# A graph attention layer on one core: the order of small index products among large products

## Chip, cores and metric

The kernel runs on one core of one Trainium2 chip. The metric is the device time of one execution in microseconds (us); lower is better. TensorE multiplies matrices, VectorE and ScalarE work on tiles, GpSimd and SyncE here mostly issue transfers (DMA) between DRAM and the core's memory.

## The reference, cut to what matters

1250 nodes with 512 features, 20000 edges sorted by destination. The part that the change touches prepares three things: per-node products that later steps gather by edge, empty tables in which the edge stage merges its sums, and index rows that say where in a tile of 128 edges the run of one destination ends.

```python
xn = _layernorm(x, axis=-1)
# inside the graph layer, node_feat = xn
x_cat = jnp.concatenate([node_feat[src], node_feat[dst], edge_feat], axis=-1)
r = x_cat @ Wr.T + br
q = (node_feat @ Wq.T + bq).reshape(n, H, D)
k = (r @ Wk.T + bk).reshape(e, H, D)
v = (r @ Wv.T + bv).reshape(e, H, D)
a = jnp.einsum('ehd,ehd->eh', q[dst], k) * scaler
amax = jax.ops.segment_max(a, dst, num_segments=n)
ae = jnp.exp(a - amax[dst])
asum = jax.ops.segment_sum(ae, dst, num_segments=n)
...
out = jax.ops.segment_sum(m, dst, num_segments=n).reshape(n, H * D)
```

After that come linear attention on the same normalised nodes and a ternary feed-forward layer.

## The kernel before, in words

The kernel is a chain of stages, each with its own instruction list for every engine: `prologue`, `edges`, `mix_and_sums`, `gnn_end`, `ffn`. Engines wait for each other only by semaphores. The change is in `prologue` alone.

Wr is used in three parts (for source, destination and edge features). Each part is multiplied with Wk and Wv into one matrix M (`fold(0)`, `fold(1)`, `fold(2)`, 96 matmuls each). All matrices are split into a high and a low half, so each product of a node tile (128 nodes) with 512 columns is 12 matmuls (`product`, L316). After `fold(0)` the loop `source(t)` makes two products for each of the 10 node tiles, with four transposes for a later tile between them (`turn`). In this stretch GpSimd loads 14 blocks of destination numbers (`load_block`, 12 edge tiles each, two buffers), and VectorE and ScalarE count in each edge tile where an edge stands in its run (`rank_group` L528, `sign_group` L430). On the same queue GpSimd clears the four merge tables (`clear_table`, L269) behind blocks 3, 5, 7 and 9.

After `fold(1)` and its eviction to M comes the destination stage, t = 0 to 9. TensorE runs `destination(t)`: a product on Wq for q, one on M for k, one on M for v, in banks 0 to 2 or 3 to 5 by turns. Behind them stand the index products of four groups of four edge tiles, `cuts(k)` for k = 4t to 4t+3: a column that marks run ends times a one-hot row matrix, 128 columns, four to a bank (6 or 7).

```python
            for t in range(NT):
                destination(t)
                for k in range(4 * t, 4 * t + 4):
                    cuts(k)
```

VectorE builds the one-hot matrices in 8 buffers (`onehot[:, i % 8, :]`, L604), so the groups k and k+2 share buffers, and group k waits for `cuts(k - 2)`. Between the groups it adds the biases to q (L610), to k (L616), forms the node's own score (L620, L623), and adds the bias to v (L626). ScalarE copies each group's bank to `cut_out` (L480), for which the store of group k-2 must have landed; GpSimd stores it to `cut_rows` (L282). SyncE stores v and q of the tile (L209, L211); they have two buffers each. At the end come two transposes, their copies, and `fold(2)`. The edge stage starts when all engines are through, GpSimd having waited for the cleared tables.

Of the kernel before, what the change touches and what calls it, by code (L numbers as in the profile page):

```python
# [106 lines left out]
def prologue(nc, x, WqT, bq, Wr, br, WkT, bk, WvT, bv, src_col, dst_col, dst_row, q_table, kv_table, v2_table, merge,  # L107
# [3 lines left out]
    with ExitStack() as ctx:  # L111
        def sb(name, shape, dt=F32):
            return ctx.enter_context(nc.sbuf_tensor(name, shape, dt))

        def sem(name):
            return ctx.enter_context(nc.semaphore(name))
# [31 lines left out]
        seg_end = sb("seg_end", [P, ET])  # L148
        is_end = sb("is_end", [P, ET])
        is_end16 = sb("is_end16", [P, ET], BF16)  # L150
        onehot = sb("onehot", [P, 8, P], BF16)
        cut_out = sb("cut_out", [1, 2, 4 * P])
        ends_out = sb("ends_out", [P, 2, P])
        banks = [ctx.enter_context(nc.psum_tensor(f"bank{i}", [P, D], F32)) for i in range(8)]
# [9 lines left out]
        q_added, kd_added, own_mul, own_sum, v2_added = (  # L164
            sem("q_added"), sem("kd_added"), sem("own_mul"), sem("own_sum"), sem("v2_added"))
        stored = [sem(f"nodes_stored{i}") for i in range(2)]
        tables_out = sem("tables_out")
# [16 lines left out]
        def wr_load(j):  # L184

            return 3 * j + 2 if j < C else (D0 + j - C if j < 2 * C else E0 + j - 2 * C)

        @block.sync
        def _(sp):
# [17 lines left out]
            def store_nodes(t):  # L207
                sp.wait_ge(v2_added, t + 1)
                sp.dma_start(v2_table[t * P:(t + 1) * P, :], v2_out[:, t % 2, :]).then_inc(stored[t % 2], 16)  # L209
                sp.wait_ge(own_sum, t + 1)  # L210
# [33 lines left out]
        def _(pool):  # L244
# [24 lines left out]
            def clear_table(i):  # L269
                pool.dma_start(merge[i].rearrange("(t p) w -> p t w", p=P),  # L270
                               empty[:, :].unsqueeze(1).to_broadcast([P, NT, TROW])).then_inc(tables_out, 16)

            pool.wait_ge(raw_in[(D0 - 3) % SLOTS], raw_landed(D0 - 3))
            pool.wait_ge(consts, 8)
            pool.dma_start(cut_rows[0:1].unsqueeze(0), empty[0:1, 0:1]).then_inc(tables_out, 16)
            for g in range(len(groups)):
                load_block(g)
                if g in (3, 5, 7, 9):
                    clear_table(g // 2 - 1)
            for k, (lo, n) in enumerate(quads):  # L280
                pool.wait_ge(cut_copied, k + 1)
                pool.dma_start(cut_rows[1 + lo * P:1 + (lo + n) * P].unsqueeze(0),  # L282
# [2 lines left out]
            pool.dma_start(end_rows[0:P * P].rearrange("(t e) -> t e", e=P), ends_out[:, 0, :]).then_inc(tables_out, 16)  # L285
            pool.dma_start(end_rows[P * P:EP].rearrange("(t e) -> t e", e=P),
                           ends_out[0:ET - P, 1, :]).then_inc(tables_out, 16)
            pool.wait_ge(tables_out, 16 * (TABLES + 3))
            pool.wait_ge(cut_stored[0], 16 * (-(-len(quads) // 2)))
            pool.wait_ge(cut_stored[1], 16 * (len(quads) // 2))  # L290

# [1 line left out]
        def _(pe):  # L293
# [22 lines left out]
            def product(out, left_hi, left_lo, t, right_hi, right_lo, cols):  # L316
                tile = slice(t * P, (t + 1) * P)
                for c in range(C):
                    pe.matmul(out, left_hi[:, c, tile], right_hi[:, c, cols], start=c == 0, stop=False)
                    pe.matmul(out, left_hi[:, c, tile], right_lo[:, c, cols], start=False, stop=False)  # L320
                for c in range(C):
                    last = pe.matmul(out, left_lo[:, c, tile], right_hi[:, c, cols], start=False, stop=c == C - 1)
                return last
# [20 lines left out]
            def destination(t):  # L344
                b = 3 * (t % 2)
                if t >= 2:
                    pe.wait_ge(q_added, t - 1)
                product(banks[b][:, :], xT_hi, xT_lo, t, Wq_hi, Wq_lo, slice(0, D)).then_inc(nodes_done, 1)
                pe.wait_ge(m_lo, 16)
                if t >= 2:  # L350
                    pe.wait_ge(kd_added, t - 1)
                product(banks[b + 1][:, :], xT_hi, xT_lo, t, M_hi, M_lo, slice(0, D)).then_inc(nodes_done, 1)
                if t >= 2:
                    pe.wait_ge(v2_added, t - 1)
                product(banks[b + 2][:, :], xT_hi, xT_lo, t, M_hi, M_lo, slice(D, 2 * D)).then_inc(nodes_done, 1)

            def cuts(k):
                lo, n = quads[k]
                pe.wait_ge(hot, lo + n)
                if k >= 2:  # L360
                    pe.wait_ge(cut_copied, k - 1)
                for i in range(n):
                    t = lo + i
                    last = pe.matmul(banks[6 + k % 2][0:1, i * P:(i + 1) * P], is_end16[:, t:t + 1], onehot[:, t % 8, :],
                                     start=True, stop=True)
                last.then_inc(cut_done, 1)

# [20 lines left out]
            fold(1)  # L388
            pe.wait_ge(lo_split, split_at(Q0 + C - 1) + 1)
            pe.wait_ge(m_lo, 9)  # L390
            for t in range(NT):
                destination(t)
                for k in range(4 * t, 4 * t + 4):
                    cuts(k)
            pe.wait_ge(cut_copied, len(quads))
            pe.transpose(banks[6][:, 0:P], seg_end[:, 0:P], ident[:, :])
            pe.transpose(banks[6][0:ET - P, P:2 * P], seg_end[:, P:ET], ident[:, :]).then_inc(cut_done, 1)
# [7 lines left out]
        def _(act):  # L405
# [67 lines left out]
            evict(1)  # L473
            split_wr(2 * C)
            split_wr(2 * C + 1)
            for k, (lo, n) in enumerate(quads):
                act.wait_ge(cut_done, k + 1)
                if k >= 2:
                    act.wait_ge(cut_stored[k % 2], 16 * (k // 2))
                act.activation(cut_out[:, k % 2, 0:n * P], banks[6 + k % 2][0:1, 0:n * P], ACT.Copy,  # L480
                               scale=NEG).then_inc(cut_copied, 1)
# [8 lines left out]
        def _(dve):  # L490
# [4 lines left out]
            def split_wr(j):  # L495
                split(wr_load(j), wr_lo[:, j % 2, :], wr_hi[:, j % 2, :])
# [97 lines left out]
            evict(1)  # L594
            split_wr(2 * C)
            split_wr(2 * C + 1)
            for t in range(NT):
                u, b = t % 2, 3 * (t % 2)
                for k in range(4 * t, 4 * t + 4):
                    lo, n = quads[k]  # L600
                    if k >= 2:
                        dve.wait_ge(cut_done, k - 1)
                    for i in range(lo, lo + n):
                        dve.tensor_scalar(onehot[:, i % 8, :], iota_row[:, :], rank[:, i:i + 1], None,  # L604
                                          ALU.is_equal).then_inc(hot, 1)
                    if k == 4 * t:
                        dve.wait_ge(nodes_done, 2 * NT + 3 * t + 1)
                        if t >= 2:
                            dve.wait_ge(stored[u], 16 * (NT // 2) + 32 * (t // 2))
                        dve.tensor_tensor(q_out[:, u, :, 0:DH], banks[b][:, :].rearrange("p (h d) -> p h d", h=H),  # L610
                                          bq_all[:, :].rearrange("p (h d) -> p h d", h=H), ALU.add).then_inc(q_added, 1)
                    if k == 4 * t + 2:
                        dve.wait_ge(nodes_done, 2 * NT + 3 * t + 2)
                        if t >= 1:
                            dve.wait_ge(own_mul, t)
                        dve.tensor_tensor(kd[:, :], banks[b + 1][:, :], bias[:, 0, :], ALU.add).then_inc(kd_added, 1)  # L616
                        dve.wait_ge(kd_added, t + 1)
                        if t >= 1:
                            dve.wait_ge(own_sum, t)
                        dve.tensor_tensor(own[:, :].rearrange("p (h d) -> p h d", h=H), kd[:, :].rearrange("p (h d) -> p h d", h=H),  # L620
                                          q_out[:, u, :, 0:DH], ALU.mult).then_inc(own_mul, 1)
                        dve.wait_ge(own_mul, t + 1)
                        dve.tensor_reduce(q_out[:, u, :, DH], own[:, :].rearrange("p (h d) -> p h d", h=H),  # L623
                                          AX.X, ALU.add).then_inc(own_sum, 1)
                dve.wait_ge(nodes_done, 2 * NT + 3 * t + 3)
                dve.tensor_tensor(v2_out[:, u, :], banks[b + 2][:, :], bias[:, 1, :], ALU.add).then_inc(v2_added, 1)  # L626
            split_wr(2 * C + 2)
            split_wr(2 * C + 3)
            evict(2)
# [1103 lines left out]
```

## Time and profile before

| | before |
|---|---|
| median of 3 runs | 1941.12 us (1935.93 to 1944.87) |
| the profiled execution | 1957.55 us, span in the trace 1955.8 us |
| TensorE busy | 1662.3 us, 85% |
| VectorE busy | 1273.3 us, 65% |
| ScalarE busy | 1027.3 us, 53% |
| GpSimd busy | 737.3 us, 38% |
| mean granted TensorE clock | 0.932 |

Busy time of an engine says how much of the span it had an instruction under way; the granted clock is the share of TensorE's full clock that the chip let it have. Shares over the whole span are means over stages with different limits, so a change in one stage is read from that stage. PE is TensorE, DVE VectorE, ACT ScalarE, POOL GpSimd, SP SyncE.

### The profile page before, as it was taken

What the parts mean: (1) busy time and instruction counts of PE and PEld (TensorE: products, weight loads), DVE (VectorE), ACT (ScalarE), POOL (GpSimd) and SP (SyncE); (2) the same over time, 40 slices, a digit from 0 to 9 for tenths busy, and PEclk for the clock granted to TensorE, in tenths of its full rate; (3) what the DMA queues carried; (4) which work ended last, traced back from release to release, by engine and by line L of the source; (5) the groups of instructions that cost most, each with busy time, mean ns of one, the idle gap of its engine ahead of it and who ended that gap; (6) DMA issues with size and microseconds to landing.
All of it is one profiled execution on the core that took longest, in us unless ns stands there. A gap on an engine that the chain in (4) does not pass through costs nothing. (4 is left out here: it accounts for less than half of the span.)

```text
span 1955.8 us, 25729 instructions
## 1 busy us (share of the span) xinstructions
PE 1662.3 (85%) x7160; PEld 1212.4 (62%) x7162; DVE 1273.3 (65%) x2943; ACT 1027.3 (53%) x3595; POOL 737.3 (38%) x727
## 2 busy tenths in 40 slices
PE   7978877999999999999999999999999467888723
PEld 6756656777777777777777777777776233443411
DVE  6764443777777777777777777777776354432588
ACT  3871111677667776776677667766776233310011
POOL 0101112455555555555555555555554000000033
PEclk9988888999999999999999999999999688999955
DMA  5860004666656666666666666666663423100001
GB/s 172 308 264 33 34 35 134 191 187 208 198 182 193 199 206 191 193 206 196 193 193 204 205 193 193 208 201 193 193 200 121 169 83 124 61 0 1 22 11 42
DMA packets 127102, 300.20 MB, mean 153 GB/s; under 512 B 29088, under 2 KB 50727, under 8 KB 126962
## 3 DMA queue, kind: packets, MB, share of 16 engines
q0 software_dynamic: 66224, 190.99, 28.3%
q1 hardware_dynamic: 60738, 107.59, 19.0%
q8 instruction: 59, 0.97, 0.2%
q14 instruction: 81, 0.66, 0.1%
HBM read 271.40 MB, written 66.58 MB: 173 GB/s over the span
## 5 line engine op out<-in xcount | busy, mean ns | idle before, releaser
L1115 ACT ACTIVATE wv<-vv,expd 128x64 f32<-128x64 f32 x1256 | 316.8, 334 | 3.2 <-ACT expd L1105 0.7
L1127 ACT ACTIVATE old<-old,expd 128x64 f32<-128x64 f32 x1256 | 307.7, 333 | 0.0
L1065 POOL DMA_INDIRECT merge<-new,put_id x157 | 159.8, 1018 | 381.3 <-DVE new L1249 352.4
L1296 PE MATMUL psV<-M_hi,efT_hi 128*128 128x512 f32 x628 | 266.1, 424 | 0.0
L1296 PE MATMUL psK<-M_hi,efT_hi 128*128 128x512 f32 x628 | 250.1, 398 | 6.5 <-ACT efT_hi L1090 6.5
L1297 PE MATMUL psV<-M_lo,efT_hi 128*128 128x512 f32 x628 | 249.8, 398 | 0.0
L1297 PE MATMUL psK<-M_lo,efT_hi 128*128 128x512 f32 x628 | 249.4, 397 | 0.0
L1036 POOL DMA_INDIRECT old<-merge,dst_id x157 | 195.8, 1247 | 49.1 <-issue 47.5
L1302 PE MATMUL psV<-M_hi,efT_lo 128*128 128x512 f32 x628 | 192.1, 407 | 0.0
L1199 DVE TENSOR_TENSOR vv<-psV,kv 128x512 f32<-128x512 f32 x157 | 108.5, 691 | 121.4 <-remote 115.8
L1036 POOL DMA_INDIRECT kv<-kv_table,src_id x157 | 155.0, 987 | 85.5 <-issue 46.9
L1206 DVE TENSOR_TENSOR wv_lo<-wv,wv_hi 128x512 fp32r<-128x512 f32 x157 | 107.9, 687 | 102.6 <-ACT wv_hi L1120 101.3
L1036 POOL DMA_INDIRECT qc<-q_table,dst_id x157 | 155.5, 991 | 47.9 <-issue 46.6
L1302 PE MATMUL psK<-M_hi,efT_lo 128*128 128x512 f32 x628 | 172.2, 396 | 0.0
L1296 PEld LDWEIGHTS psV<-M_hi,efT_hi 128*128 128x128 f32 x628 | 118.5, 189 | 40.3 <-issue 17.1
L1296 PEld LDWEIGHTS psK<-M_hi,efT_hi 128*128 128x128 f32 x628 | 118.9, 189 | 36.2 <-ACT efT_hi L1090 6.9
L1297 PEld LDWEIGHTS psK<-M_lo,efT_hi 128*128 128x128 f32 x628 | 118.8, 189 | 28.6
L1302 PEld LDWEIGHTS psK<-M_hi,efT_lo 128*128 128x128 f32 x628 | 118.5, 189 | 29.0
L1297 PEld LDWEIGHTS psV<-M_lo,efT_hi 128*128 128x128 f32 x628 | 119.1, 190 | 21.8
L1097 ACT ACTIVATE runsT<-psT 128x16 f32<-128x16 f32 (+1 forms) x79 | 14.5, 183 | 220.0 <-PE psT L1335 220.0
L1302 PEld LDWEIGHTS psV<-M_hi,efT_lo 128*128 128x128 f32 x628 | 112.5, 189 | 21.6
L1523 POOL MEMSET onem<- 128x128 f32 x1 | 0.2, 205 | 321.7 <-POOLq L1374 321.7
(261 smaller groups left out, 3200.9 us busy)
## 6 DMA issues: line engine op xcount, KB each, us to landing
efT<-in_ef_turned_dram SPq DMA_DIRECT2D x78, 512.0 KB
merge<-empty POOLq DMA_DIRECT2D x4, 2640.0 KB, 15.0
rows<-merge SPq DMA_DIRECT2D x40, 264.0 KB, 3.7
row_block<-dst_rows POOLq DMA_DIRECT2D x13, 768.0 KB, 7.1
dst_line<-dst_rows SPq DMA_DIRECT2D x78, 128.0 KB
end_line<-end_rows SPq DMA_DIRECT2D x78, 128.0 KB
kv_table<-kv_out SPq DMA_DIRECT2D x10, 512.0 KB, 5.6
raw<-in_L_gnn_Wr_dram SPq DMA_DIRECT2D x12, 256.0 KB, 5.1
```

Source lines behind the costliest of these rows:

```text
L1036: pool.indirect_dma_start(out=out, out_offset=None, in_=table[:, :], in_offset=bass.IndirectOffsetOnAxis(ap=ids[:, t:t + 1], axis=0)).then ...
L1065: pool.indirect_dma_start(out=merge[2 * (p % 2) + u][:, :], out_offset=bass.IndirectOffsetOnAxis(ap=put_id[:, t:t + 1], axis=0), in_=new[p ...
L1097: act.activation(runsT[:, 0:n, :], turned_s[:, 0:n, :], ACT.Copy).then_inc(runs_copied, 1)
L1115: act.activation(wv[:, u, h * DH:(h + 1) * DH], vv[:, u, h * DH:(h + 1) * DH], ACT.Copy, scale=expd[p % 2][:, u, 0, h:h + 1]).then_inc(wv_ ...
L1127: act.activation(rows, rows, ACT.Copy, scale=expd[p % 2][:, u, 1, h:h + 1]).then_inc(old_scaled, 1)
L1199: dve.tensor_tensor(vv[:, u, :], psV[u][:, :], kv[p % 2][:, u, D:2 * D], ALU.add).then_inc(v_added, 1)
L1206: dve.tensor_tensor(wv_lo[:, u, :], wv[:, u, :], wv_hi[:, u, :].bitcast(F32), ALU.subtract).then_inc(wv_lo_ready, 1)
L1296: pe.matmul(out[:, :], efT_hi[b][:, u, c, :], Me_hi[:, c, col:col + D], start=c == 0, stop=False)
L1297: pe.matmul(out[:, :], efT_hi[b][:, u, c, :], Me_lo[:, c, col:col + D], start=False, stop=False)
L1302: last = pe.matmul(out[:, :], efT_lo[b][:, u, c, :], Me_hi[:, c, col:col + D], start=False, stop=c == C - 1)
L1523: pool.memset(onem[:, :], 1.0).then_inc(cst, 1)
```

## The change

Three edits in `prologue`. (1) TensorE's order in the destination stage: the products are dealt out singly, with one or two groups of index products between them, and the q product of tile t+2 is made after the v product of tile t. (2) The one-hot rows have 16 buffers, four groups, and VectorE's order follows: a group waits for the group four before it. Two semaphores of the own score become one. (3) The four table clears are issued by ScalarE on its own DMA queue, ahead of the copies of groups 0, 6, 12 and 18, with a semaphore of their own.

```diff
-        onehot = sb("onehot", [P, 8, P], BF16)
+        onehot = sb("onehot", [P, 16, P], BF16)
...
+        def destination_at(kind, t):
+            before = 2 * NT + 2 * t + min(t + 2, NT)
+            return {"q": 2 * NT + t + 1 + 2 * max(t - 1, 0), "k": before + 1, "v": before + 2}[kind]
...
             for g in range(len(groups)):
                 load_block(g)
-                if g in (3, 5, 7, 9):
-                    clear_table(g // 2 - 1)
...
-            pool.wait_ge(tables_out, 16 * (TABLES + 3))
+            pool.wait_ge(tables_out, 16 * 3)
+            pool.wait_ge(cleared, 16 * TABLES)
...
-            for t in range(NT):
-                destination(t)
-                for k in range(4 * t, 4 * t + 4):
-                    cuts(k)
+            destination_q(0)
+            pe.wait_ge(m_lo, 12)
+            destination_q(1)
+            pe.wait_ge(m_lo, 16)
+            for t in range(NT):
+                if t >= 1:
+                    cuts(4 * t - 2)
+                    cuts(4 * t - 1)
+                destination_k(t)
+                cuts(4 * t)
+                destination_v(t)
+                cuts(4 * t + 1)
+                if t + 2 < NT:
+                    destination_q(t + 2)
+            cuts(len(quads) - 2)
+            cuts(len(quads) - 1)
...
+            act.wait_ge(consts, 8)
             for k, (lo, n) in enumerate(quads):
+                if k % 6 == 0 and k // 6 < TABLES:
+                    act.dma_start(merge[k // 6].rearrange("(t p) w -> p t w", p=P),
+                                  empty[:, :].unsqueeze(1).to_broadcast([P, NT, TROW])).then_inc(cleared, 16)
                 act.wait_ge(cut_done, k + 1)
...
+            def one_hots(k):
+                lo, n = quads[k]
+                if k >= 4:
+                    dve.wait_ge(cut_done, k - 3)
...
+            one_hots(0)
+            one_hots(1)
+            add_q(0)
+            one_hots(2)
+            one_hots(3)
+            for t in range(NT):
+                if t + 1 < NT:
+                    add_q(t + 1)
+                own_scores(t)
+                if t + 1 < NT:
+                    one_hots(4 * t + 4)
+                    one_hots(4 * t + 5)
+                add_v2(t)
+                if t + 1 < NT:
+                    one_hots(4 * t + 6)
+                    one_hots(4 * t + 7)
```

`add_q`, `own_scores` and `add_v2` hold the same five VectorE operations as before, each with a wait for its product by the count of `destination_at`; `add_q` and now `add_v2` wait for the stores of tile t-2.

## Rows read from the trace of the kernel before

**Rows 1.** Busy time by stretch: us, then each engine, clock, DMA share, GB/s.

```profile
40.00:80.00 40.00, 39.02 (x185) 32.15 (x184) 29.66 (x134) 26.37 (x114) 4.11 (x6) 1.00 0.64 229
143.75:293.81 150.06, 117.64 (x519) 89.43 (x520) 69.50 (x216) 25.20 (x48) 19.34 (x40) 0.84 0.10 34
```

**Rows 2.** Waits, 149 to 293 us: total us, times, longest.

```profile
DVE onehot L604 <- PE bank L364: 42.7, 10, 4.5
...
PE bank L364 <- DVE onehot L604: 31.3, 20, 2.4
```

**Rows 3.** Timeline of TensorE between tiles 0 and 1: start us, us.

```profile
154.49 0.61 PE L364 MATMUL bank<-onehot,is_end 128*1 128x128 bf16 x8
...
158.67 0.39 PE L364 MATMUL bank<-onehot,is_end 128*1 128x128 bf16 x4 [2.44 <-DVE onehot L604]
158.98 0.79 PE L319 MATMUL bank<-Wq_hi,xT_hi 128*128 128x512 f32 x1
```

**Rows 4.** Groups by line, 149 to 293 us.

```profile
L604 DVE TENSOR_SCALAR onehot<-iota_row,rank 128x128 bf16<-128x128 f32 x157 | 34.1, 280 | 42.7 <-PE bank L364 42.7
L319 PE MATMUL bank<-M_hi,xT_hi 128*128 128x512 f32 x80 | 31.6, 395 | 0.0
...
L319 PE MATMUL bank<-Wq_hi,xT_hi 128*128 128x512 f32 x36 | 23.0, 640 | 0.0
L480 ACT ACTIVATE cut_out<-bank 1x512 f32<-1x512 f32 (+1 forms) x40 | 22.0, 574 | 123.8 <-PE bank L364 105.6 <-DMA cut_rows<-cut_out 18.2
...
L282 POOL DMA_DIRECT2D cut_rows<-cut_out x40 | 19.3, 485 | 136.3 <-ACT cut_out L480 136.2
...
L610 DVE TENSOR_TENSOR q_out<-bank,bq_all 128x512 f32<-128x512 f32 x10 | 6.9, 690 | 35.7 <-PE bank L322 35.7
```

**Rows 5.** Waits, 55 to 149 us.

```profile
DVE junk L534 <- DMA row_block<-dst_rows: 12.8, 5, 5.8
...
PE bank L319 <- DVE xT_lo L525: 4.7, 1, 4.7
```

**Rows 6.** Transfers: KB each, us to landing; windows 60:150, 57:62 twice, 98:104 twice.

```profile
merge<-empty POOLq DMA_DIRECT2D x4, 2640.0 KB, 15.0
...
row_block<-dst_rows POOLq DMA_DIRECT2D x1, 768.0 KB, 6.0
kv_table<-kv_out SPq DMA_DIRECT2D x1, 512.0 KB, 3.2
...
row_block<-dst_rows POOLq DMA_DIRECT2D x1, 768.0 KB, 10.8
kv_table<-kv_out SPq DMA_DIRECT2D x1, 512.0 KB, 8.5
```

**Rows 7.** Timeline of TensorE, source stage to the first destination products.

```profile
76.33 0.60 PE L331 MATMUL bank<-ident,raw 128*128 128x128 f32 x4
...
82.23 0.60 PE L331 MATMUL bank<-ident,raw 128*128 128x128 f32 x4
...
94.62 0.60 PE L331 MATMUL bank<-ident,raw 128*128 128x128 f32 x4
...
105.98 0.39 PE L305 MATMUL bank<-W_hi,wr_hi 128*128 128x512 f32 x1
...
143.78 0.76 PE L319 MATMUL bank<-Wq_hi,xT_hi 128*128 128x512 f32 x1 [9.48 <-DVE M_lo L502]
...
148.92 0.40 PE L319 MATMUL bank<-M_hi,xT_hi 128*128 128x512 f32 x1
```

**Rows 8.** Stores of the destination stage and its end on the timeline.

```profile
q_table<-q_out SPq DMA_DIRECT2D x10, 260.0 KB, 2.4
...
cut_rows<-cut_out POOLq DMA_DIRECT2D x39, 2.0 KB, 1.5
...
291.83 0.22 PE L364 MATMUL bank<-onehot,is_end 128*1 128x128 bf16 x1 [1.86 <-DVE onehot L604]
...
293.81 0.76 PE L305 MATMUL bank<-W_hi,wr_hi 128*128 128x512 f32 x1 [0.72 <-ACT ends_out L484]
```

More of the change, by code:

```diff
@@ L163, in prologue @@
         nodes_done, ks_copied, vs_copied = sem("nodes_done"), sem("ks_copied"), sem("vs_copied")
-        q_added, kd_added, own_mul, own_sum, v2_added = (
-            sem("q_added"), sem("kd_added"), sem("own_mul"), sem("own_sum"), sem("v2_added"))
+        q_added, kd_added, own_step, v2_added = sem("q_added"), sem("kd_added"), sem("own_step"), sem("v2_added")
         stored = [sem(f"nodes_stored{i}") for i in range(2)]
-        tables_out = sem("tables_out")
+        tables_out, cleared = sem("tables_out"), sem("cleared")
         block_in = [sem(f"block_in{i}") for i in range(2)]
@@ L209, in store_nodes @@
                 sp.dma_start(v2_table[t * P:(t + 1) * P, :], v2_out[:, t % 2, :]).then_inc(stored[t % 2], 16)
-                sp.wait_ge(own_sum, t + 1)
+                sp.wait_ge(own_step, 2 * t + 2)
                 sp.dma_start(q_table[t * P:(t + 1) * P, :],
@@ L267, in load_block @@
                                dst_rows[lo * P:(lo + n) * P].unsqueeze(0).to_broadcast([P, n * P])).then_inc(block_in[g % 2], 16)
-            def clear_table(i):
-                pool.dma_start(merge[i].rearrange("(t p) w -> p t w", p=P),
-                               empty[:, :].unsqueeze(1).to_broadcast([P, NT, TROW])).then_inc(tables_out, 16)
             pool.wait_ge(raw_in[(D0 - 3) % SLOTS], raw_landed(D0 - 3))
@@ L342, in source, with destination_q, destination_k, destination_v @@
                 product(banks[b + 1][:, :], xT_hi, xT_lo, t, M_hi, M_lo, slice(D, 2 * D)).then_inc(nodes_done, 1)
-            def destination(t):
-                b = 3 * (t % 2)
+            def destination_q(t):
                 if t >= 2:
                     pe.wait_ge(q_added, t - 1)
-                product(banks[b][:, :], xT_hi, xT_lo, t, Wq_hi, Wq_lo, slice(0, D)).then_inc(nodes_done, 1)
-                pe.wait_ge(m_lo, 16)
+                product(banks[3 * (t % 2)][:, :], xT_hi, xT_lo, t, Wq_hi, Wq_lo, slice(0, D)).then_inc(nodes_done, 1)
+            def destination_k(t):
                 if t >= 2:
                     pe.wait_ge(kd_added, t - 1)
-                product(banks[b + 1][:, :], xT_hi, xT_lo, t, M_hi, M_lo, slice(0, D)).then_inc(nodes_done, 1)
+                product(banks[3 * (t % 2) + 1][:, :], xT_hi, xT_lo, t, M_hi, M_lo, slice(0, D)).then_inc(nodes_done, 1)
+            def destination_v(t):
                 if t >= 2:
                     pe.wait_ge(v2_added, t - 1)
-                product(banks[b + 2][:, :], xT_hi, xT_lo, t, M_hi, M_lo, slice(D, 2 * D)).then_inc(nodes_done, 1)
+                product(banks[3 * (t % 2) + 2][:, :], xT_hi, xT_lo, t, M_hi, M_lo, slice(D, 2 * D)).then_inc(nodes_done, 1)
             def cuts(k):
@@ L363, in cuts @@
                     t = lo + i
-                    last = pe.matmul(banks[6 + k % 2][0:1, i * P:(i + 1) * P], is_end16[:, t:t + 1], onehot[:, t % 8, :],
+                    last = pe.matmul(banks[6 + k % 2][0:1, i * P:(i + 1) * P], is_end16[:, t:t + 1], onehot[:, t % 16, :],
                                      start=True, stop=True)
@@ L596, in _ @@
             split_wr(2 * C + 1)
-            for t in range(NT):
[L598 to L626, printed above, removed]
@@ new lines, in one_hots, with add_q @@
+            def one_hots(k):
+                lo, n = quads[k]
+                if k >= 4:
+                    dve.wait_ge(cut_done, k - 3)
+                for i in range(lo, lo + n):
+                    dve.tensor_scalar(onehot[:, i % 16, :], iota_row[:, :], rank[:, i:i + 1], None,
+                                      ALU.is_equal).then_inc(hot, 1)
+            def add_q(t):
+                u = t % 2
+                dve.wait_ge(nodes_done, destination_at("q", t))
+                if t >= 2:
+                    dve.wait_ge(stored[u], 16 * (NT // 2) + 32 * (t // 2))
+                dve.tensor_tensor(q_out[:, u, :, 0:DH], banks[3 * u][:, :].rearrange("p (h d) -> p h d", h=H),
+                                  bq_all[:, :].rearrange("p (h d) -> p h d", h=H), ALU.add).then_inc(q_added, 1)
@@ new lines, in own_scores @@
+            def own_scores(t):
+                u = t % 2
+                dve.wait_ge(nodes_done, destination_at("k", t))
+                if t >= 1:
+                    dve.wait_ge(own_step, 2 * t - 1)
+                dve.tensor_tensor(kd[:, :], banks[3 * u + 1][:, :], bias[:, 0, :], ALU.add).then_inc(kd_added, 1)
+                dve.wait_ge(kd_added, t + 1)
+                dve.wait_ge(q_added, t + 1)
+                if t >= 1:
+                    dve.wait_ge(own_step, 2 * t)
+                dve.tensor_tensor(own[:, :].rearrange("p (h d) -> p h d", h=H), kd[:, :].rearrange("p (h d) -> p h d", h=H),
+                                  q_out[:, u, :, 0:DH], ALU.mult).then_inc(own_step, 1)
+                dve.wait_ge(own_step, 2 * t + 1)
+                dve.tensor_reduce(q_out[:, u, :, DH], own[:, :].rearrange("p (h d) -> p h d", h=H),
+                                  AX.X, ALU.add).then_inc(own_step, 1)
@@ new lines, in add_v2 @@
+            def add_v2(t):
+                u = t % 2
+                dve.wait_ge(nodes_done, destination_at("v", t))
+                if t >= 2:
+                    dve.wait_ge(stored[u], 16 * (NT // 2) + 32 * (t // 2))
+                dve.tensor_tensor(v2_out[:, u, :], banks[3 * u + 2][:, :], bias[:, 1, :], ALU.add).then_inc(v2_added, 1)
+            one_hots(0)
[3 more added lines that the diff above has]
+            one_hots(3)
+            for t in range(NT):
+                if t + 1 < NT:
[8 more added lines that the diff above has]
+                    one_hots(4 * t + 7)
```

## The prediction

> **What bounds the kernel now.** I read first the busy shares by stretch. In the destination stage, 143.75 to 293.81 us, TensorE is busy for 118 of 150 us at a granted clock of 0.84, while VectorE has 70 us of work, ScalarE 25 and GpSimd 19; the DMA engines run at a tenth [rows 1]. Nobody but TensorE is near full, so TensorE's waits and its clock set this stage. The waits say whom it waits for: 31.3 us in 20 waits before index products, for the one-hot rows of VectorE, which itself waited 42.7 us in 10 waits for index products [rows 2]. That is a loop: eight row buffers hold two groups, so groups 4t+2 and 4t+3 can only be built after groups 4t and 4t+1 were used, and those stand behind all three products of tile t. The timeline shows one turn of it: the eight ready products at 154.49, then idle, the last group at 158.67 after 2.44 us of waiting, the next tile's first product at 158.98 [rows 3]. The reader should see a second loss in the grouped rows: a matmul on Wq takes 640 ns, the same shape on M 395 ns [rows 4]. The first after each pause runs at the lower of the two clock levels (1.2 GHz), the others at 2.4 GHz.
>
> The stage before it, the source tiles and the second fold, stops twice, for 4.7 us on VectorE's low part and again inside the fold; VectorE was late because its rank work waited for a block of destination rows from DRAM (VectorE 12.8 us in all) [rows 5]. Those loads share GpSimd's queue with four table clears of 2640 KB, each 15.0 us to landing; a block load takes 6.0 us with no clear about and up to 10.8 behind one [rows 6].
>
> **The change, part by part.**
>
> *Clears leave the source stage.* Issued from ScalarE at groups 0, 6, 12 and 18, they no longer stand ahead of block loads. Source tiles follow each other at 82.23 − 76.33 = 5.90 us when nothing stops; the stretch with the first stop took 94.62 − 82.23 = 12.39 us, so 6.5 us come back, its slow restart included. The last stretch before the fold, 94.62 to 105.98, is 11.36 us with four products and one set of transposes, 5.90 has two products and one set: a product at full clock is (11.36 − 5.90)/2 = 2.73 us, a matmul 0.2275 us. The fold has 96 of them, 21.8 us; with 0.2 for the last one's way out 22.0; it took from 105.98 to 134.30 (143.78 less the wait of 9.48), 28.3 us: 6.3 us come back [rows 7]. Behind it come ScalarE's splits and 37 sign passes, which start when the second round of the fold ends, so they move with it. Sum 12.8 us. Bounds: nothing, if 6.0 us of a block load is still too late (it is asked for a tile and two copies ahead, 5.90 + 2 × 0.57 = 7.0 us, so 1 us to spare), and 12.8.
>
> *Index products dealt out, four groups of rows kept.* No instruction is removed: 30 products, 157 index products, 157 one-hots, 50 vector operations and 40 copies remain, as do the SyncE stores and GpSimd's 40 issues. What goes is the pause. In the new order the groups used in tile t are 4t−2, 4t−1, 4t and 4t+1, and VectorE has built each at least one product earlier. I laid the engines side by side over one tile, with k ending at 0: v ends at 3.1, its index group at 3.5, the next q at 6.2, two groups at 6.9, the next k at 9.7. VectorE does its three operations from 0 to 2.1 (0.69 each), a group to 3.0 (16 rows cost 16 × 0.217 = 3.5 us a tile), waits for the index group at 3.5 and builds the next to 4.4, adds v to 5.1, waits for 6.5, builds two groups to 8.3, adds q to 9.0 and is back 0.7 us before the next k. It has 3.5 + 5 × 0.69 = 6.9 us of work in 9.7 [rows 4]; TensorE never finds it late.
>
> TensorE's time then: the first q product after a pause, 148.92 − 143.78 = 5.14 us, as now [rows 7]; 29 products of 2.73, 79.2 us; 40 groups. A group of four takes 158.98 − 158.67 = 0.31 us [rows 3], and a set of four transposes with both changeovers 5.90 − 5.46 = 0.44 us; I take 0.37, so 14.8. Then the tail: now 293.81 − 291.83 = 2.0 us from the last index product to the third fold; with three groups close together at the end one more copy and store stand in it, 3.0 us [rows 8]. Sum 5.1 + 79.2 + 14.8 + 3.0 = 102.1 against 293.81 − 143.78 = 150.0: 47.9 us less. Bounds: 0.31 a group and a tail of 2.0 give 3.4 more; and if the short tail lets the third fold begin at full clock, another 5.14 − 2.73 = 2.4.
>
> *The clock* is part of that sum: from 40 to 80 us, products with transposes between them, the granted clock is 1.00 [rows 1], and it was 0.84 only where pauses stand. The Trainium skill ("TensorE: Matmul & The Clock Gate", HAM oscillation) says that bursts with waits between them pay for the return to the full clock each time; by that rule nothing in the sum changes while the pauses are gone, and the trace agrees (640 against 395 ns). It counts only TensorE's activity, and says nothing of a stationary operand one column wide, which is the doubt that I price below.
>
> *Clears in the destination stage.* Issue: the nearest row is GpSimd's 485 ns for a cut store, and ScalarE has 40 copies of 574 ns [rows 4]; even twice that four times lies in ScalarE's idle time, 125 of 150 us. Their bytes collide with two small transfers [rows 8]. A cut store (1.5 us now) must land before the second next copy, and TensorE needs that copy two groups later: one tile, 9.7 us, less two copies and an issue, leaves 7.5 us. A q store (2.4 us) must land before the q addition two tiles on, which by the schedule above comes when it would have landed; but that addition can be 7 us late before TensorE notices, and VectorE has 2.8 us a tile to catch up. Under clears a kv store took 8.5 us where it took 3.2 without [rows 6]. So from nothing to about 1 us a clear; I take nothing, and without that slack a clear would cost the whole difference, 5 us. The Trainium skill ("DMA: Bandwidth & Descriptors", Queues, rings and completion order) says that each DMA engine turns from queue to queue packet by packet; by it the delay would be that of a packet and the sum the same. The 8.5 us speak for more than that. The first clear starts before any index product and meets nothing.
>
> *Edges and all that follows* hold the same instructions and shift with the start. Total 12.8 + 47.9 = 60.7 us. The profiled execution is 1957.6 us (span 1955.8 and 1.8 around it), so 1896.9 after; the median of the unprofiled runs is 16.4 us lower and I take the saving over whole: 1941.1 − 60.7 = 1880.4 us.
>
> **Rivals.**
> 1. *Stores stuck behind the clears.* If a cut store has to wait for a whole clear, 15.0 us, TensorE stops for 15.0 − 7.5 and restarts slowly, 7.5 + 2.4 = 9.9 us at each of three clears: 30 us back, 1910 us. For it: kv stores slowed to 8.5 us; against: 8.5 is not 15, and the queues are different.
> 2. *The block loads stay late.* Then 12.8 us are missing: 1893 us. For it: only 1 us to spare; against: 6.0 is less than 7.0, and only the loads behind a clear rose to 10.8.
> 3. *The change doesn't break the loop.* Some wait keeps one pause a tile, say half of today's 31.3/10 = 3.1 us of index waits plus a slow restart of 2.41, 4 us × 9: 36 us missing, 1916 us. Against: the schedule above, tight only on VectorE with 0.7 us.
> 4. *Other side: the clock stays low.* If index products with one stationary column, now after every product, keep TensorE at 1.2 GHz, 29 products cost 2.41 us more each, 70 us, and 40 groups between nothing and their 0.31 more, taken as 0.17, 7 us: 60.7 − 77 is 16 us slower, 1957 us. At 2.65 us for a slow product with its groups, 23 of them eat the gain and 27 of 29 make it measurably slower. Against: transposes in that place leave the clock at 1.00, and 0.37 us in 3.1 is little idleness.
>
> **How the numbers follow.** A measurement of this kernel can tell about 0.5%, 10 us, from no change. Forecast 0.76, rival 1 0.08, rival 2 0.07, rival 3 0.05, rival 4 0.03, and 0.01 for no change. The likeliest case alone reaches from 1941 − 66.5 = 1875 to about 1887; with the scatter of the runs shown, a quarter of a percent, 1870 to 1892. Adding rival 2 and most of the way to rival 1: 1866 to 1904. Only rival 4 and no change lie outside faster: faster 0.95, same 0.02, slower 0.03.
>
> **What would show it.** In the profile after: no wait of TensorE on one-hot rows, a destination stage of about 102 us with a granted clock above 0.95, matmuls on Wq at the 395 ns of the others; no stop near 83 and 110 us and a destination stage that begins about 13 us earlier; cut stores that may land in up to 8 us but no stop on copies. I am wrong if the clock in that stage is 0.9 or lower, if TensorE waits for ScalarE's copies near a clear, or if block loads still hold up VectorE.

## The result and the profile after

The changed kernel takes 1885.5 us (median of 4 runs, 1883.8 to 1887.9) against 1939.3 us for the kernel before (1935.9 to 1944.9): a ratio of 0.9719, 95% interval 0.9702 to 0.9736, 53.8 us faster. The forecast was 1880 us, 60.7 us faster. In all comparisons below each kernel is set against the kernel before on the same chip. The later runs were made on three chips: the kernel before takes 1899.2 us where the e runs were made, 1943.8 us for the f runs and 1898.3 us for the g runs. So ratios are compared across chips, not times. The stages of the prologue can be compared as they are: the difference lies behind them, since from the first product of the edge stage to the end of the span the traces show 1566 to 1572 us in the e and g runs and 1610 to 1614 us in the f runs.

The view that groups busy time by stretch gives the two stages, with the same columns as [rows 1]:

```profile
130.55:239.24 108.69, 102.66 (x520) 74.74 (x520) 69.35 (x216) 25.31 (x48) 19.58 (x40) 0.99 0.39 145
57.00:130.55 73.55, 65.11 (x300) 53.59 (x298) 56.87 (x321) 70.67 (x321) 6.34 (x12) 0.98 0.67 227
```

The destination stage has the same work for VectorE, ScalarE and GpSimd as before and takes 108.7 us instead of 150.0; TensorE is busy for 103 of them, and its granted clock is 0.99 instead of 0.84. It starts at 130.55 us instead of 143.78. Together, before rounding, these make 54.6 us. The edge stage's first product starts 55.6 us earlier; the last 1.0 us comes from the third fold, whose first matmul stood 30.9 us ahead of that product and now stands 29.9 us ahead of it.

```profile
324.74 0.80 PE L1296 MATMUL psK<-M_hi,efT_hi 128*128 128x512 f32 x1 [6.50 <-ACT efT_hi L1090]
...
269.13 0.80 PE L1338 MATMUL psK<-M_hi,efT_hi 128*128 128x512 f32 x1 [6.25 <-issue]
```

(The first line is of the kernel before, the second of the kernel after.) The spans of the two profiled executions differ by more, 69.7 us: as said ahead, the profiled execution of before was 16.4 us over its median, and the rest of the 69.7 lies behind 324.74 us, in work that did not change.

The waits from 128 to 250 us (total us, times, longest), against [rows 2]:

```profile
ACT cut_out L497 <- DMA cut_rows<-cut_out: 23.1, 9, 6.0
DVE q_out L627 <- DMA q_table<-q_out: 21.2, 6, 8.5
...
DVE onehot L619 <- PE bank L365: 7.8, 7, 1.8
...
PE bank L409 <- ACT cut_out L497: 2.8, 1, 2.8
PE bank L365 <- DVE onehot L619: 2.0, 2, 1.5
```

TensorE's 31.3 us of waiting for one-hot rows are 2.0. One wait is new, that of VectorE for q stores (21.2 us), and one is longer than before, that of ScalarE for stores of index rows (23.1 us, 18.2 before). Nearly all of this lies beside TensorE's work.

The timeline of TensorE, against [rows 7]: the transposes keep their distance of 5.90 us past 82.88, and the fold starts at 100.14 instead of 105.98.

```profile
82.88 0.60 PE L330 MATMUL bank<-ident,raw 128*128 128x128 f32 x4
88.78 0.60 PE L330 MATMUL bank<-ident,raw 128*128 128x128 f32 x4
100.14 0.39 PE L304 MATMUL bank<-W_hi,wr_hi 128*128 128x512 f32 x1
...
130.55 0.77 PE L318 MATMUL bank<-Wq_hi,xT_hi 128*128 128x512 f32 x1 [8.45 <-DVE M_lo L519]
...
134.87 0.39 PE L318 MATMUL bank<-Wq_hi,xT_hi 128*128 128x512 f32 x1
```

The rest of that timeline, inside a tile and at the end, against [rows 3, 8]:

```profile
202.75 0.38 PE L365 MATMUL bank<-onehot,is_end 128*1 128x128 bf16 x4
203.06 0.50 PE L318 MATMUL bank<-M_hi,xT_hi 128*128 128x512 f32 x1
203.40 0.40 PE L319 MATMUL bank<-M_lo,xT_hi 128*128 128x512 f32 x1
203.64 0.40 PE L318 MATMUL bank<-M_hi,xT_hi 128*128 128x512 f32 x1
...
205.04 1.08 PE L321 MATMUL bank<-M_hi,xT_lo 128*128 128x512 f32 x4
206.05 0.38 PE L365 MATMUL bank<-onehot,is_end 128*1 128x128 bf16 x4
206.36 0.50 PE L318 MATMUL bank<-Wq_hi,xT_hi 128*128 128x512 f32 x1
...
209.36 0.61 PE L365 MATMUL bank<-onehot,is_end 128*1 128x128 bf16 x8
209.90 0.50 PE L318 MATMUL bank<-M_hi,xT_hi 128*128 128x512 f32 x1
...
238.09 0.33 PE L409 MATMUL bank<-ident,seg_end 128*128 128x128 f32 x1 [2.78 <-ACT cut_out L497]
...
239.24 0.49 PE L304 MATMUL bank<-W_hi,wr_hi 128*128 128x512 f32 x1 [0.72 <-ACT ends_out L501]
```

From one product to the next with a lone group between them it is 206.36 − 203.06 = 3.30 us, with a pair 209.90 − 206.36 = 3.54. Against a product of 2.73 us a lone group costs 0.57 and a pair 0.81. Only 0.31 of the 0.57 is the way from the first index product to the next product. The rest lies inside the product: its first matmul takes 0.34 us to the second (203.06 to 203.40) instead of 0.2275, the next seven 0.234 each, and its last four, up to the first index product, 206.05 − 205.04 = 1.01 us. Between two products of the kernel before, with nothing between them, these four take 0.90 us:

```profile
181.05 1.07 PE L322 MATMUL bank<-M_hi,xT_lo 128*128 128x512 f32 x4
181.95 0.39 PE L319 MATMUL bank<-M_hi,xT_hi 128*128 128x512 f32 x1
```

So a lone group costs 0.31 + 0.11 + 0.05 + 0.10 = 0.57 us.

Transfers, KB each and us to landing, from 168 to 176 us, a stretch in which the third clear runs (against [rows 6, 8]):

```profile
merge<-empty ACTq DMA_DIRECT2D x1, 2640.0 KB, 11.6
q_table<-q_out SPq DMA_DIRECT2D x1, 260.0 KB, 9.6
v_table<-v_out SPq DMA_DIRECT2D x1, 256.0 KB, 6.9
cut_rows<-cut_out POOLq DMA_DIRECT2D x3, 2.0 KB, 5.9
```

The slow q store reaches TensorE once, through VectorE:

```profile
178.96 0.69 DVE L627 TENSOR_TENSOR q_out<-bank,bq_all 128x512 f32<-128x512 f32 x1 [8.52 <-DMA q_table<-q_out]
...
182.53 0.38 PE L365 MATMUL bank<-onehot,is_end 128*1 128x128 bf16 x4 [1.45 <-DVE onehot L619]
```

### The profile page after: what moved, and what is told of

Its sections match the earlier page's. It is cut to its first block and busy times, and to the rows that moved or that the text cites. A ratio compares the mean times of both kernels' runs of the same rounds, so it can differ in the third digit from the quotient of the medians.

```text
span 1886.1 us, 25733 instructions
## 1 busy us (share of the span) xinstructions
PE 1648.3 (87%) x7162; PEld 1198.9 (64%) x7162; DVE 1272.6 (67%) x2943; ACT 1027.2 (54%) x3595; POOL 732.7 (39%) x723
## 5 line engine op out<-in xcount | busy, mean ns | idle before, releaser
L1241 DVE TENSOR_TENSOR vv<-psV,kv 128x512 f32<-128x512 f32 x157 | 108.5, 691 | 107.3 <-remote 99.7
L1248 DVE TENSOR_TENSOR wv_lo<-wv,wv_hi 128x512 fp32r<-128x512 f32 x157 | 107.9, 687 | 101.3 <-ACT wv_hi L1162 98.4
```

Source lines behind the costliest of these rows:

```text
L1241: dve.tensor_tensor(vv[:, u, :], psV[u][:, :], kv[p % 2][:, u, D:2 * D], ALU.add).then_inc(v_added, 1)
L1248: dve.tensor_tensor(wv_lo[:, u, :], wv[:, u, :], wv_hi[:, u, :].bitcast(F32), ALU.subtract).then_inc(wv_lo_ready, 1)
```

## Experiments

First the destination stage of every profiled run, read from its timeline (first q product to first matmul of the third fold), the part of it from the first q product to the next product, and the ratio of times to the kernel before:

| run | stage starts, us | stage, us | of that the first q product, us | ratio (95% interval) |
|---|---|---|---|---|
| before | 143.8 | 150.0 | 5.1 | 1 |
| after | 130.6 | 108.7 | 4.3 | 0.9719 (0.9702 to 0.9736) |
| e1 clears only | 130.5 | 149.5 | 5.3 | 0.9921 (0.9906 to 0.9936) |
| e2 order only | 144.5 | 108.1 | 5.2 | 0.9764 (0.9749 to 0.9779) |
| e3 eight buffers | 129.1 | 109.7 | 5.2 | 0.9708 (0.9695 to 0.9721) |
| e4 old order, 16 buffers | 143.3 | 110.4 | 5.3 | 0.9781 (0.9766 to 0.9796) |
| f0 after again | 131.1 | 108.8 | 4.4 | 0.9718 (0.9704 to 0.9732) |
| f1 groups in pairs | 131.5 | 108.3 | 5.3 | 0.9715 (0.9697 to 0.9732) |
| f2 four copy buffers | 129.1 | 107.3 | 5.3 | 0.9700 (0.9685 to 0.9714) |
| f3 16 buffers and clears, old order | 130.8 | 114.6 | 5.3 | 0.9742 (0.9728 to 0.9756) |
| g1 clears early, own queue | 145.3 | 107.9 | 4.8 | 0.9780 (0.9759 to 0.9801) |
| g2 clears late, GpSimd's queue | 129.6 | 110.3 | 5.3 | 0.9708 (0.9689 to 0.9726) |
| g3 index products twice | 131.7 | 115.9 | 5.3 | 0.9759 (0.9741 to 0.9777) |
| g4 all together | 130.8 | 102.6 | 4.2 | 0.9684 (0.9668 to 0.9700) |

Two columns show how finely these single traces can be read. Kernels whose code is the same up to the stage start it at 129.1 to 131.7 us (clears moved out of the source stage) or at 143.3 to 145.3 us (clears in it), so a start is good to 1 to 2 us. And the first q product, which always follows the long wait for M, takes 4.2 to 5.3 us whatever was changed, with a granted clock of 0.63 over it in the kernel after and 0.50 in e2: it is a matter of when the clock rises, and up to 1 us of a difference between two stages can be this alone. The two lines of e2:

```profile
144.51 0.77 PE L323 MATMUL bank<-Wq_hi,xT_hi 128*128 128x512 f32 x1 [9.54 <-DVE M_lo L520]
...
149.75 0.40 PE L323 MATMUL bank<-Wq_hi,xT_hi 128*128 128x512 f32 x1
```

**The two halves alone.** e1 is the kernel before with the third edit (its completions counted on a semaphore that is idle by then); e2 the kernel after without it.

```diff
 e1, against before
-                if g in (3, 5, 7, 9):
-                    clear_table(g // 2 - 1)
...
+                if k % 6 == 0 and k // 6 < TABLES:
+                    act.dma_start(merge[k // 6]...).then_inc(cleared, 16)
```

> The kernel before with the third edit alone: clears from ScalarE at groups 0, 6, 12, 18, old order, 8 buffers. Theory (the two gains add up): the destination stage starts 13 us earlier and is itself unchanged at 150 us, so 13 us faster, about 1926. Rival (clears cost in the destination stage what they gave before): in the old order ScalarE's copies already wait for stores, so three clears of about 10 us each stretch that stage by 3 us or more each; 1930 or above.

> The kernel after with the clears back on GpSimd's queue in the source stage. Theory (a group of index products between products costs about 0.5 us, not the 0.37 taken, and clears cost the stage nothing): the destination stage takes 107 to 109 us without any clear in it, the two source stops are back, 41 to 43 us faster than before, about 1898. Rival (the 6.6 us by which the stage was longer than forecast come from the clears): the stage takes 102 to 103 us, 47 us faster, about 1892.

e1 is 14.8 us faster, e2 44.0 us faster. That is 0.79% and 2.36%, together 3.15%, where the kernel after has 2.81%. The traces show a smaller excess: the edge stage starts 15.0 us earlier in e1 and 42.3 in e2, together 57.3, and 55.6 earlier in the kernel after; what makes up the rest is not shown. In e1 the destination stage starts 13.3 us earlier and takes 149.5 us: the clears cost the old order nothing measurable. In e2 it takes 108.1 us with no clear in it. That is 0.6 us less than in the kernel after, but e2's first q product took 0.9 us more; without that product it is 102.9 against 104.4 us. So the clears cost the dealt order 1.5 us, which is the one stop of 1.45 us shown above and missing in e2. Most of the 6.6 us over the forecast is not the clears', and the theory of a dearer group stands.

**Is it the order or the buffers?** e3 is the kernel after with 8 buffers; e4 the kernel before with 16.

```diff
 e3, against after
-        onehot = sb("onehot", [P, 16, P], BF16)
+        onehot = sb("onehot", [P, 8, P], BF16)
-                if k >= 4:
-                    dve.wait_ge(cut_done, k - 3)
+                if k >= 2:
+                    dve.wait_ge(cut_done, k - 1)
 e4, against before
-        onehot = sb("onehot", [P, 8, P], BF16)
+        onehot = sb("onehot", [P, 16, P], BF16)
-                    if k >= 2:
-                        dve.wait_ge(cut_done, k - 1)
+                    if k >= 4:
+                        dve.wait_ge(cut_done, k - 3)
```

> The kernel after with 8 one-hot buffers instead of 16, each group waiting for the one two before it. Theory A (the dealt order is what counts; VectorE then runs later but has 2.8 us a tile to spare): within 3 us of the kernel after, 1885 to 1888. Theory B (the four groups are needed too): TensorE waits for rows once a tile, 1 us or more, and the clock dips; 10 us or more slower than the kernel after, over 1895.

> The kernel before with 16 one-hot buffers alone: old order of products, clears where they were. Theory A (the buffers alone break the loop: all 16 rows of a tile can be built before its v product ends, and a burst of four groups waits only for two copies, about 1 us a tile): a period of about 10.5 us a tile, some 38 us faster, about 1901. Theory B (dealing out is needed): the pause stays for half or more, VectorE builds after its additions, 15 us faster or less, 1925 or above.

Either half is enough. e3 is at the ratio of the kernel after within the intervals, with a stage 1.0 us longer, 0.8 of it in the first q product. e4 brings 41.6 us by more buffers and a later wait alone: its stage is 110.4 us, 39.6 us shorter than before. It has no clears in its stage, so its match is e2, which is 41.9 us shorter. One turn of its timeline on TensorE:

```profile
185.33 0.61 PE L364 MATMUL bank<-onehot,is_end 128*1 128x128 bf16 x8
186.48 0.86 PE L364 MATMUL bank<-onehot,is_end 128*1 128x128 bf16 x8 [0.55 <-DVE onehot L604]
...
195.73 0.61 PE L364 MATMUL bank<-onehot,is_end 128*1 128x128 bf16 x8
```

Two groups, a wait of 0.55 us (put down to the rows by the profile), two groups, and the next tile: 10.40 us a tile, where the dealt order takes 3.30 + 3.30 + 3.54 = 10.14.

**What dealing out buys.** f3 has 16 buffers and the moved clears but the old order, f0 is the kernel after on the same chip.

```diff
 f3, against before: the edits of e1 and of e4
```

> The kernel after, unchanged, as the measure for the three beside it on the same chip: ratio to the kernel before 0.970 to 0.974.

> The kernel before with the clears from ScalarE and 16 one-hot buffers, but the old order of products: everything of the change except the dealing out. Theory (dealing out adds little once the buffers are there): the two gains add, ratio 0.970 to 0.975, within 3 us of the kernel after. Rival (bursts of four groups need quick stores, which the clears slow down): the stage grows by 5 us or more over the 110.4 us that it takes without clears in it, and the run is 7 us or more behind the kernel after.

f3 is 5.8 us slower than f0 (1893.4 against 1887.6); the intervals of their ratios overlap only from 0.9728 to 0.9732. Its stage is 5.9 us longer than that of f0, 0.9 of it in the first q product, and 4.2 us longer than that of e4. The timeline shows where most of the 4.2 come from, a burst under the second clear:

```profile
165.61 0.86 PE L360 MATMUL bank<-onehot,is_end 128*1 128x128 bf16 x8 [2.28 <-ACT cut_out L480]
```

Four groups in a burst need two copies at once, and these wait for stores slowed by the clear. The stop and the slower product behind it cost 3.3 us. Dealt out, the same clears cost 1.5 us. The theory's 3 us were too few; the rival was right in direction, and its bounds of 5 and 7 us were a little high.

**Where the missing microseconds are.** f1 moves the group between k and v behind v; f2 gives the copies four buffers; g3 makes each index product twice into the same place.

```diff
 f1
                 destination_k(t)
-                cuts(4 * t)
                 destination_v(t)
+                cuts(4 * t)
                 cuts(4 * t + 1)
...
 f2 (copies go to the idle row_block; two more semaphores)
-                if k >= 2:
-                    act.wait_ge(cut_stored[k % 2], 16 * (k // 2))
+                if k >= 4:
+                    act.wait_ge(cut_stored[k % 4], stored_before[k % 4] + 16 * (k // 4))
 g3
-                for i in range(n):
+                for i in [j for j in range(n) for _ in range(2)]:
```

> The kernel after with the group between k and v moved behind v, so that groups stand two and two. Theory (the missing time is the changeover: a lone group moves the next product by 0.57 us, a pair by 0.81 in the trace of the kernel after): 2 x 0.57 + 0.81 = 1.95 us a tile become 1.62, 3 us less in the stage, 106 us. Rival (the cost lies in the index products themselves): no change, within 1 us.

> The kernel after with four buffers for the copies of index rows instead of two (in the row blocks, idle by then), each copy waiting for the store four groups before. Theory (the wait of 2.8 us ahead of the two last transposes is the copy of the last group waiting for a store): the stage loses 2 us, and ScalarE's 23 us of waits for stores go; stage 106 to 107 us, the run 2 us faster. If the third fold then starts at full clock, another 1 to 2 us. Rival (the waits on stores under the clears also delay TensorE): 4 us or more faster.

> The kernel after with every index product made twice into the same place (same result). Theory (of the 0.57 us that a lone group costs, 4 x 0.055 are its matmuls and the rest is a changeover that comes once a group): 157 more at 0.055 us, 8.6 us more in the stage, 117 us, group 0.79 us. Rival (each index product costs a quarter of the 0.57 us): 157 x 0.14, 20 us more.

In g3 the distance between products with a lone group, doubled, is:

```profile
154.06 0.50 PE L318 MATMUL bank<-M_hi,xT_hi 128*128 128x512 f32 x1
...
157.00 0.61 PE L365 MATMUL bank<-onehot,is_end 128*1 128x128 bf16 x8
157.54 0.50 PE L318 MATMUL bank<-Wq_hi,xT_hi 128*128 128x512 f32 x1
...
165.01 0.50 PE L318 MATMUL bank<-M_hi,xT_hi 128*128 128x512 f32 x1
```

157.54 − 154.06 = 3.48 us, 0.18 more than with a single set, and a whole tile takes 165.01 − 154.06 = 10.95 us, 0.81 more for 16 more index products: 0.05 us each. The stage is 7.1 us longer than that of f0 (8.6 expected), with 0.9 us more in the first q product and without the stop of 1.45 us. So of 0.57 us a lone group has 0.2 in its matmuls and some 0.35 in the changeover.

f1 agrees inside a tile but not in the sum. Its tile takes 168.60 − 158.85 us:

```profile
158.85 0.61 PE L365 MATMUL bank<-onehot,is_end 128*1 128x128 bf16 x8
159.39 0.50 PE L318 MATMUL bank<-M_hi,xT_hi 128*128 128x512 f32 x1
...
168.60 0.61 PE L365 MATMUL bank<-onehot,is_end 128*1 128x128 bf16 x8
```

9.75 us is 0.39 less than 10.14, as the changeover theory says, and over the stage some 3 us. But the first two q products took 1.3 us more than in f0, at the lower clock, and under the fourth clear TensorE waited 2.2 and 0.4 us for rows, where f0 has one stop of 1.45. The stage is 0.4 us shorter (3 us expected), and there is no measurable gain. In f2 the wait of 2.78 us ahead of the transposes is 0.36, and ScalarE waits for no store any more. From the last index product to the fold it is 1.7 us instead of 4.15, a gain of 2.4 us; the first q product took back 0.9, and the stage is 1.5 us shorter. The run's gain over f0 is the size of the measurement's width. The stop of 1.45 us stays in f2, so it does not come from ScalarE's copies.

**Is it the queue or the bytes?** g1 puts the clears back into the source stage, on ScalarE's own queue; g2 leaves them late, on the queue of the index stores.

```diff
 g1 (ScalarE, source stage; no clears in the destination stage)
                 sign_group(t)
+                if t in (1, 3, 5, 7):
...
+                    act.dma_start(merge[t // 2]...).then_inc(cleared, 16)
...
 g2 (GpSimd instead of ScalarE, destination stage)
             for k, (lo, n) in enumerate(quads):
+                if k % 6 == 0 and k // 6 < TABLES:
+                    pool.dma_start(merge[k // 6]...).then_inc(cleared, 16)
                 pool.wait_ge(cut_copied, k + 1)
```

> The kernel after with the clears back in the source stage, but issued by ScalarE on its own queue, behind the sign passes of blocks 1, 3, 5 and 7, so at about the times of before. Theory A (the block loads were late because they stood behind a clear on GpSimd's queue): no stop near 83 and 110 us, the destination stage starts near 131 us as in the kernel after, ratio to before about 0.972. Theory B (the bytes count, whichever the queue): block loads take 8 us or more against 7.0 us of room, stops of 1 to 5 us stay and the stage starts at 135 us or later; ratio 0.974 to 0.978.

> The kernel after with the clears issued by GpSimd in the destination stage, ahead of the stores of groups 0, 6, 12 and 18, on the queue of these stores. Theory A (a small store behind a clear on one queue waits for all of it, 8 us or more): ScalarE's copies and with them TensorE stop once at each of three clears for 1 to 5 us; stage 112 to 120 us. Theory B (the queue does not matter, only the shared engines): like the kernel after, 108 to 110 us.

Waits of g1 from 55 to 135 us:

```profile
DVE junk L553 <- DMA row_block<-dst_rows: 17.5, 4, 7.4
ACT junk_act L449 <- DMA row_block<-dst_rows: 17.2, 4, 5.5
...
PE bank L318 <- DVE xT_lo L544: 5.3, 2, 2.9
PE bank L304 <- ACT kv_out L474: 3.4, 1, 3.4
```

The clears are issued from 61.6 to 109.0 us, where the kernel before has them from 63.3 to 104.9. On a queue of their own they do as much harm: a block load takes 9.7 us (median), VectorE waits 17.5 us for block loads (12.8 before, [rows 5]), and the destination stage starts at 145.3 us, no earlier than before. The bytes at that time were the cost, not their place in a queue. g2 says nearly the same from the other side: with the clears on the queue of the small stores the longest of these takes 9.6 us to landing, 6.2 in the kernel after. ScalarE waits 37.2 us for stores instead of 23.1, and TensorE stops once, 1.66 us, for a copy. But the stage is 110.3 us, with 0.9 us more in the first q product than the kernel after, and the ratio is that of the kernel after within the intervals. Moving the clears in time is what counts; which engine issues them hardly does.

**A better version.** g4 joins f1 and f2 and issues two clears before the first index product and two behind the last one.

> A version meant to beat the kernel after: groups in pairs, four buffers for the copies, two clears issued before the first index product and two behind the last one. Theory (gains add: 0.4 us of pairs, 1.5 of the copies, 2.2 of the stop on rows under a clear, 0.6 of the clears): stage 104 to 106 us, 3 to 5 us faster than the kernel after, ratio 0.969 to 0.970. Rival: the two late clears, 20 us of transfers, delay the start of the edge stage beyond the fold, and the gain is lost.

Its stage is 102.6 us (104 to 106 expected, and it had a short first q product), its ratio 0.9684 against 0.9718 of f0, 0.34% or some 6.5 us less than the kernel after; the intervals just part. It has the lowest ratio, but its interval overlaps those of f2, e3 and g2, so it is not shown to be faster than f2. With no clear between index products TensorE has no stop longer than 0.55 us between the first product and the transposes, and the pairs' gain stays. TensorE at the end:

```profile
231.31 0.33 PE L410 MATMUL bank<-ident,seg_end 128*128 128x128 f32 x1 [0.52 <-ACT row_block L502]
...
233.40 0.76 PE L305 MATMUL bank<-W_hi,wr_hi 128*128 128x512 f32 x1 [1.65 <-ACT ends_out L508]
...
264.69 0.79 PE L1345 MATMUL psK<-M_hi,efT_hi 128*128 128x512 f32 x1 [6.40 <-ACT efT_hi L1139]
```

The 1.65 us instead of 0.72 ahead of the fold go with ScalarE issuing the two late clears before its last copies. From the third fold to the first edge product it is 31.3 us, against 29.9 in the kernel after. That is the fold's slower start: over its first 6 us the granted clock is 0.50, and 0.72 in the kernel after. The wait ahead of the edge stage is about the same (6.4 and 6.25 us), so the late clears' transfers are hidden by the fold.

## Why the prediction was right, step by step

**The clears' departure**, 12.8 us forecast: 13.2 us in the kernel after, 13.3 in e1, and 12.1 to 14.7 over all runs with the clears moved. Both stops are gone and the fold runs through. The size was right. The reason given for it, block loads standing behind a clear on GpSimd's queue, was wrong in its second half: g1 took the clears off that queue and lost the gain. Loads were late because the engines moved 2640 KB more beside them. The 1 us to spare held: a block load now takes 5.9 us (median). VectorE still waits 4.4 us for block loads, but TensorE doesn't stop for it.

**The loop**: right. VectorE's and TensorE's waits for each other are gone. But the text treated the dealt order and the four groups as one thing. e3 and e4 show two independent ways to break the loop: 8 buffers in the dealt order give 40.4 of the 41.3 us, 16 buffers in the old order 39.6 of the 41.9 that the stage gains without clears in it, and 35.4 of 41.3 with them (f3).

**TensorE's time in the stage**, 102.1 us forecast, 108.7 measured. The step that was mis-sized most is the group term, 0.37 us × 40 = 14.8. In a full tile it is 2 × 0.57 + 0.81 = 1.95 us, 0.49 a group. The tail was 239.24 − 235.09 = 4.15 us instead of 3.0, the waits on rows and a copy 2.5 us instead of none; the first q product took 4.3 instead of 5.1. With 79.2 for the other 29 products that leaves 108.7 − 4.3 − 79.2 − 2.5 − 4.15 = 18.5 us for the groups of the whole stage, which in its last two tiles stand closer together: 0.46 each, 3.7 us more than forecast. So 3.7 + 2.5 + 1.2 − 0.8 = 6.6 us. Of the 2.5 us of waits 1.45 are the third clear's stop; the others (0.54 and 0.55) stand in e2 too, which has no clears in the stage. The 0.8 us gained in the first q product are luck: most other runs have 5.2 or 5.3 there. The upper value, four transposes with both changeovers at 0.44, is no bound for index products: a pair of groups costs 0.81 but a lone one 0.57, for the three parts shown above.

**VectorE's schedule** had the q addition arrive just when the q store lands, with 7 us until TensorE notices. Under the third clear the q store took 9.6 us, VectorE stood for 8.5, and TensorE noticed with one stop of 1.45 us, within the "nothing to about 1 us a clear" of the text. That chain of three is read from the order of events; e2, without clears in the stage, has neither the stop nor the wait on q stores, and f2, where ScalarE waits for no store, has both. **Clears in this stage**: taken at nothing, 1.5 us measured (after less e2, both without the first q product). The slack of a cut store is 8.1 us by the terms named for it, 9.7 − 2 × 0.57 − 0.49, and not 7.5; nothing here depends on the difference. **The issue**: 0.37 us each on ScalarE. **The clock**: 0.99, so the rival with one-column operands at 1.2 GHz is out. At the end, after the tail's waits, the third fold starts at the lower level: its first matmuls follow each other at 0.43 us up to 242.94, the later ones at 0.23, and the granted clock of its first 6 us is 0.72. The Trainium skill ("TensorE: Matmul & The Clock Gate", HAM oscillation) says that bursts with waits between them pay for the return to the full clock each time, and the trace agrees.

**The rivals.** Stores stuck for a whole clear: they took at most 6.2 us, inside the 7.5 of slack and less than the 8.5 us of the kv stores. The Trainium skill ("DMA: Bandwidth & Descriptors", Queues, rings and completion order) has each DMA engine turn from queue to queue packet by packet. The prediction took from it a delay of one packet; the trace has 5.9 against 1.5 us for a 2 KB store, so that estimate was too low. Block loads that stay late: no. A pause that stays: no.

**The signs.** Of the signs named, the early start and the clock came as said. The stage was 108.7 us and not about 102, and TensorE has two waits on one-hot rows, 2.0 us. It also waits for copies, 0.55 and 2.78 us, but at the end of the stage and not near a clear (e2 has both without clears).

The forecast saving of 60.7 us was 6.9 too large. Up to the edge stage the traces account for some 5 of it: 6.6 too much for the stage, less 0.4 more than forecast from the clears' departure and 1.0 gained in the third fold, which was not forecast. The other 1.8 is the 55.6 us of the two traces against the 53.8 of the medians, and is not explained.

## What to carry to other kernels

Where two engines wait for each other in turn, count the buffers between them before rewriting an order: here twice the buffers gave 39.6 of 41.9 us. Dealing small work out among large work was then the second step, worth 2 us in a quiet stage and 5 where small stores were slow, since it gives each of them time. Bulk transfers belong into a stretch where the DMA engines idle (a share of 0.10 before the change); a queue of their own in a full stretch gained nothing here.

## What was not expected of the hardware

A lone group of four small matmuls (bf16, one stationary column, 128 moving) between products of 512 columns costs 0.57 us, of which only 0.2 are its own matmuls (g3); the first large matmul after it needs 0.34 us to the next instead of 0.23, and the last four before the next group 1.01 us instead of 0.90. A 2 KB store beside a clear of 2640 KB on another queue takes 5.9 us instead of 1.5 (up to 6.2), and on the clear's own queue up to 9.6 (g2). A clear itself took 15.0 us among other traffic and 8.4 to 11.6 in the emptier stage.
